# Last batch's tail in a gated cross-attention and mixture-of-experts kernel: the residual update moved from VectorE to ScalarE and GpSimd

## The chip, the cores and the metric

The kernel runs on one core of a Trainium2 chip, as one launch. The metric is the device time in microseconds (us), as the median of a few runs. TensorE is called PE below, VectorE DVE, ScalarE ACT, GpSimd POOL and SyncE SP, as the profile calls them.

## What is computed

Four batches of 512 tokens with 512 features go through a gated cross-attention to 64 context tokens, and then through a router and a mixture of 8 experts, of which each token takes 2. The part around the change is the end of the attention block and the start of the router:

```python
delta = ctx @ Wo.T + bo                      # [512 tokens, 512]
delta = rs * delta
delta = (delta - mean) / sqrt(var + EPS) * ln_gamma + ln_beta
x1 = x + tanh(g_xattn) * delta               # residual: stored, the output starts from it
h = (x1 - mean(x1)) / sqrt(var(x1) + EPS)    # second layer norm: stored, experts gather it
logits = h @ gate_weight.T                   # [2048, 8], top 2 of 8 follow
out = x1 + tanh(g_ffn) * experts(h)          # only after all 2048 tokens are routed
```

## The kernel before

The kernel is written engine by engine, with semaphores; each engine runs its list in the order written. Batches 0 to 3 go through attention in a software pipeline, in which the output of batch b-1 is finished while batch b's scores are computed. The last batch (`LAST`, 3) has nothing behind it: its four tiles of 128 tokens (t = 0 to 3) go through a **tail**, in which the engines hand each tile on to each other:

1. PE makes `delta` in a PSUM bank (`last_o_product`), then is done with it.
2. DVE, in `update_and_residual(n, u, r, last)`: for tile u, `bn_stats` and `bn_aggr` of `delta`, then `dh = (delta - mean) * gamma` (semaphore `dgam`; this is the line L459). For tile r, one `scalar_tensor_tensor` (L435) `xr = dh * rs + xs` (`x1_done`), then `bn_stats` (L439) and the variance of `xr` (`hvar`, L449). `xs` holds x + beta. One call does u = t and r = t - 1.
3. POOL: `inverse_delta(t)` is a power, `rs = (var + eps)^-1/2` (L812); `inverse_h(t)` is the same for the second norm (`rsh`, L816) and `nmh = -mean * rsh` (L819, semaphore `hbias`). `last_x_beta(t)` adds beta to x in `xs` (L891).
4. ACT, `normalise_h`: `dh = xr * rsh + nmh` (L1040, `h_done`).
5. PE, `h_transposes`: four 128x128 transposes of `dh` (L1409, `h_tr`).
6. ACT, `h_copy`: the transposed tile from PSUM to `ht` (L1047, `h_ev`).
7. PE, `router`: eight small matmuls `ht` by `gate_w` (L1415, `lg_mm`); a copy of the 8 logits follows (`keep_logits`, on DVE for the last batch, L464, on ACT for the others, L1052).

Between these steps PE runs `stay_busy(n)`: n transposes of the identity into a bank that nobody reads (L1303), 6 between a tile's transposes and its router, 12 behind each router but the last, 22 behind the last.

Behind the tail comes the routing. DVE picks the two best experts of each token in a chain of small instructions on 128x128 elements (from L643 on). ACT first splits three of expert 0's weight pieces (`first_gu`, L1216), whose weights were loaded meanwhile, and then computes the exponential that DVE's `wden` (L661) waits for. Slots are placed, the first rows are gathered by DMA, and then 37 slot tiles go through the experts' matmuls (L259) in a loop that takes the rest of the time.

SP stores x1 and h of each tile as they are done. Its `stores(n)` waits for `x1_done` and `h_done` in turn.

Of the kernel before, what the change touches and what calls it, by code (L numbers as in the profile page):

```python
# [4 lines left out]
ALU = mybir.AluOpType  # L5
ACT = mybir.ActivationFunctionType
# [9 lines left out]
NB = 4  # L16
# [27 lines left out]
def flamingo_gated_block(nc, x, ctx_t, mask, w_attn, b_cols, b_rows, gates, gate_t, w_exp, out):  # L44
    st = ExitStack()
    with st:
# [3 lines left out]
        def sem(name):  # L50
            return st.enter_context(nc.semaphore(name))
# [177 lines left out]
        o_l2, last_xb = sem("o_lo_second_half_done"), sem("last_x_with_beta")  # L229
        d_mm, dstats, dmean, dvar, drstd, dgam, xb_done, x1_done = (sem(n) for n in  # L230
# [54 lines left out]
        def _(sp):  # L285
# [13 lines left out]
            def stores(n):  # L299
                for t in range(TT):  # L300
                    sp.wait_ge(x1_done, n * TT + t + 1)
                    sp.dma_start(out_rows[n * TT + t], xr[:, t, :]).then_inc(x1_store[t], 16)
                    sp.wait_ge(h_done, n * TT + t + 1)
                    sp.dma_start(h_rows[n * TT + t], dh[:, t, :]).then_inc(h_store[t], 16)
# [24 lines left out]
            stores(LAST)  # L329
# [21 lines left out]
        def _(dve):  # L351
# [72 lines left out]
            def update_and_residual(n, u, r, last=False):  # L424
                delta = None if u is None else tail_bank[u] if last else bank[2 + u % 2]

                if r is not None:
                    dve.wait_ge(dgam, n * TT + r + 1)
                    dve.wait_ge(drstd, n * TT + r + 1)
                    if last:  # L430
                        dve.wait_ge(last_xb, r + 1)
                        dve.wait_ge(x1_store[r], 16 * NB)
                    else:
                        dve.wait_ge(xb_done, n * TT + r + 1)
                    dve.scalar_tensor_tensor(out=xr[:, r, :], in0=dh[:, r, :], scalar=rs[:, r:r + 1],  # L435
                                             in1=(xs if last else xr)[:, r, :],
                                             op0=ALU.mult, op1=ALU.add).then_inc(x1_done, 1)
                    dve.wait_ge(x1_done, n * TT + r + 1)
                    dve.bn_stats(st6h[:, r, :], xr[:, r, :]).then_inc(hstats, 1)  # L439
# [169 lines left out]
            for t in range(TT + 1):  # L609
                update_and_residual(LAST, t if t < TT else None, t - 1 if t > 0 else None, last=True)  # L610
# [155 lines left out]
        def _(pool):  # L766
# [43 lines left out]
            def inverse_delta(n, t):  # L810
                pool.wait_ge(dvar, n * TT + t + 1)
                pool.tensor_tensor(rs[:, t:t + 1], ve[:, t:t + 1], mhalf[:, 0:1], ALU.pow).then_inc(drstd, 1)  # L812
# [105 lines left out]
            for t in range(TT + 1):  # L918
                if t < TT:
                    inverse_delta(LAST, t)  # L920
                if t >= 1:
                    inverse_h(LAST, t - 1)
                if t < 2:
                    last_x_beta(t + 2)
# [62 lines left out]
        def _(act):  # L987
# [49 lines left out]
            def normalise_h(n, t):  # L1037
                act.wait_ge(x1_done, n * TT + t + 1)
                act.wait_ge(hbias, n * TT + t + 1)
                act.activation(dh[:, t, :], xr[:, t, :], ACT.Identity, scale=rsh[:, t:t + 1],  # L1040
                               bias=nmh[:, t:t + 1]).then_inc(h_done, 1)
# [169 lines left out]
            keep_logits(LAST - 1, 2)  # L1211
            h_copy(LAST - 1, 3)
# [9 lines left out]

            for t in range(TT):
                normalise_h(NB - 1, t)
                h_copy(NB - 1, t, tail=True)
# [70 lines left out]
        def _(pe):  # L1296
# [264 lines left out]
            for t in range(TT):  # L1561
                h_transposes(NB - 1, t, tail=True)
                stay_busy(6, tail_bank[0])
                router(NB - 1, t, tail=True)
                if t < TT - 1:
                    stay_busy(12, tail_bank[0])
# [120 lines left out]
```

## Time and profile before

| | us |
|---|---|
| median of 3 runs | 956.95 (953.62 to 959.67) |
| the profiled execution | 953.08 |
| its span, first to last instruction | 951.3 |
| PE busy | 904.9 (95%) |
| DVE busy | 432.6 (45%) |
| ACT busy | 383.4 (40%) |
| POOL busy | 267.8 (28%) |
| mean granted TensorE clock | 0.987 of full |

The page divides the span into 40 slices of 23.8 us. The tail, 219 to 240 us, lies in the tenth slice and the first part of the eleventh, and the routing in the rest of the eleventh and the twelfth. PE's busy digits are 7 to 9 in the first ten slices, 6 in the eleventh, and 9 from the twelfth on, but for the last. The granted clock, in tenths of full speed (9 is 90% or more), is 7 in the eleventh slice and in the last one, and 9 in all others. Busy time of PE contains the identity transposes, so it doesn't say how much of it is work.

### The profile page before, as it was taken

The page shows a single profiled execution, that of the slowest core. Times are in us where ns is not written, and L with a number is a line of the kernel's source. Part 1 is how long each engine was busy: PE and PEld are TensorE (multiplying, and loading weights), DVE is VectorE, ACT ScalarE, POOL GpSimd, SP SyncE. Part 2 cuts the span into 40 slices and gives each one's busy share as a digit, 9 for nine tenths or more (in the row PEclk, how much of TensorE's full clock was granted, in tenths as well). Part 3 has the DMA queues.
Part 4 walks back from the last instruction along what each step waited for, and adds up shares of the span by engine and source line. Part 5 has one row for each costly group of instructions (what it writes and reads, how often), then busy time and mean ns, then how long its engine had stood idle before and what let it go on. Part 6 is the DMA issues. An engine that isn't in the chain of part 4 may idle for free.

```text
span 951.3 us, 14769 instructions
## 1 busy us (share of the span) xinstructions
PE 904.9 (95%) x4369; PEld 726.9 (76%) x4370; DVE 432.6 (45%) x802; ACT 383.4 (40%) x740; POOL 267.8 (28%) x330
## 2 busy tenths in 40 slices
PE   7978999999699999999999999999999999999994
PEld 7746777778578888888888888888888888888883
DVE  5658868577871221721621635422532172136111
ACT  4485757543332222622622625322622262235221
POOL 6136555564412112212212212211311221212211
PEclk9999999999799999999999999999999999999997
DMA  8210222108272112631631543611551263121121
GB/s 315 90 45 1 78 100 77 56 34 314 99 288 44 23 22 37 208 109 33 203 117 33 189 131 110 221 22 22 170 161 22 37 213 103 33 33 22 33 33 22
DMA packets 27812, 92.90 MB, mean 98 GB/s; under 512 B 5457, under 2 KB 5457, under 8 KB 21137
## 3 DMA queue, kind: packets, MB, share of 16 engines
q1 hardware_dynamic: 18576, 72.03, 20.2%
q0 software_dynamic: 8640, 20.62, 11.8%
q8 instruction: 9, 0.15, 0.1%
q14 instruction: 11, 0.08, 0.0%
q10 hardware_dynamic: 576, 0.02, 0.0%
HBM read 73.98 MB, written 18.68 MB: 97 GB/s over the span
## 4 chain that ended last, share of the span: by engine, by line
PE 80%; issue 6%; POOL 5%; DVE 4%; ACT 3%; DMA 1%; DVEq 0%; SPq 0%; POOLq 0%; ACTq 0%
PE bank L259 71%; PE bank L1612 3%; PE bank L1598 2%; POOL ex_lo L824 2%; POOL o_lo L804 1%; DMA raw<-in_w_attn 1%; PE bank L1415 1%; PE bank L1303 1%; POOL xr L808 1%; ACT g_hi L1216 1%; PE bank L1409 1%; PE bank L1351 0%; DVE tok_tile L691 0%; DMA xg<-h_rows,slot_idx 0%; PE bank L1331 0%
## 5 line engine op out<-in xcount | busy, mean ns | idle before, releaser
L259 PE MATMUL bank<-g_hi,gt_hi 128*128 128x512 f32 x592 | 237.5, 401 | 0.9 <-DVE gt_lo L717 0.9
L259 PE MATMUL bank<-g_lo,gt_hi 128*128 128x512 f32 x592 | 234.1, 395 | 0.0
L259 PE MATMUL bank<-g_hi,gt_lo 128*128 128x512 f32 x592 | 234.1, 395 | 0.0
L747 DVE TENSOR_TENSOR hid<-silu,bank 128x256 f32<-128x256 f32 x148 | 61.4, 419 | 306.9 <-ACT silu L1268 306.9
L1268 ACT ACTIVATE silu<-bank 128x256 f32<-128x256 f32 x148 | 56.5, 382 | 253.0 <-PE bank L259 253.0
L966 POOL COPY g_idx<-slot_idx 128x1 int32 x37 | 6.9, 185 | 470.3 <-ACT w_nxt L1282 470.3
L259 PEld LDWEIGHTS bank<-g_hi,gt_lo 128*128 128x128 f32 x592 | 111.3, 188 | 27.0
L259 PEld LDWEIGHTS bank<-g_hi,gt_hi 128*128 128x128 f32 x592 | 111.3, 188 | 26.3 <-issue 1.1
L259 PEld LDWEIGHTS bank<-g_lo,gt_hi 128*128 128x128 f32 x592 | 111.4, 188 | 25.0
L259 PE MATMUL bank<-dn_hi,hd_hi 128*128 128x512 f32 x296 | 126.8, 428 | 0.0
L259 PE MATMUL bank<-dn_hi,hd_lo 128*128 128x512 f32 x296 | 116.9, 395 | 0.0
L259 PE MATMUL bank<-dn_lo,hd_hi 128*128 128x512 f32 x296 | 116.4, 393 | 0.0
L615 DVE TENSOR_TENSOR g_lo<-raw,g_hi 128x2048 fp32r<-128x2048 f32 x32 | 72.4, 2286 | 9.8 <-ACT g_hi L1216 9.7
L730 DVE TENSOR_TENSOR hd_lo<-bank,hd_hi 128x256 fp32r<-128x256 f32 x148 | 58.8, 418 | 36.2 <-ACT hd_hi L1251 36.2
L975 POOL DMA_INDIRECT out_rows<-y_sb,s_idx x37 | 59.1, 1597 | 41.7 <-ACT y_sb L1289 36.1
L1251 ACT ACTIVATE hd_hi<-bank 128x256 fp32r<-128x256 f32 x148 | 52.5, 384 | 42.1 <-PE bank L1612 42.1
L259 PEld LDWEIGHTS bank<-dn_hi,hd_lo 128*128 128x128 f32 x296 | 55.9, 189 | 13.8
L259 PEld LDWEIGHTS bank<-dn_lo,hd_hi 128*128 128x128 f32 x296 | 56.1, 189 | 8.1
L259 PEld LDWEIGHTS bank<-dn_hi,hd_hi 128*128 128x128 f32 x296 | 55.8, 189 | 8.0 <-issue 0.2
L824 POOL TENSOR_TENSOR ex_lo<-ex,ex_hi 128x512 fp32r<-128x512 f32 x32 | 43.8, 1387 | 63.9 <-ACT ex_hi L1064 30.3
L1216 ACT ACTIVATE g_hi<-raw 128x2048 fp32r<-128x2048 f32 x32 | 61.0, 1912 | 0.0
L946 POOL DMA_INDIRECT xg<-h_rows,g_idx x38 | 50.8, 1337 | 30.7 <-POOL g_idx L966 30.1
(236 smaller groups left out, 1284.8 us busy)
## 6 DMA issues: line engine op xcount, KB each, us to landing
raw<-in_w_exp SPq DMA_DIRECT2D x48, 1024.0 KB, 5.3
xs<-in_x SPq DMA_DIRECT2D x4, 1024.0 KB, 6.3
out_rows<-xr SPq DMA_DIRECT2D x16, 256.0 KB, 2.1
h_rows<-dh SPq DMA_DIRECT2D x16, 256.0 KB, 2.1
raw<-in_w_attn SPq DMA_DIRECT2D x3, 1024.0 KB, 14.0
xr<-in_x SPq DMA_DIRECT2D x3, 1024.0 KB, 5.8
raw<-in_w_attn SPq DMA_DIRECT2D x4, 256.0 KB, 7.2
rows<-in_b_rows SPq DMA_DIRECT2D x1, 1024.0 KB, 17.6
```

The source lines that it names most:

```text
L259: mm = eng.matmul(psum, a(k), b(k), start=(first and k == 0 and j == 0), stop=(last and k == n - 1 and j == 2))
L615: dve.tensor_tensor(dst.rearrange("p k n -> p (k n)"), raw[:, p, :], f32(hi.rearrange("p k n -> p (k n)")), ALU.subtract).then_inc(done, 1)
L730: dve.tensor_tensor(hd_lo[:, 2 * p:2 * p + 2, :].rearrange("p k n -> p (k n)"), bank[4 + p % 2][:, 0:256], f32(hd_hi[:, 2 * p:2 * p + 2, : ...
L747: dve.tensor_tensor(hid[:, p, :], silu[:, p, :], bank[p][:, 256:512], ALU.mult).then_inc(hid_done, 1)
L824: pool.tensor_tensor(ex_lo[:, s % RING, :], ex[:, s % 2, :], f32(ex_hi[:, s % RING, :]), ALU.subtract).then_inc(e_l, 1)
L946: pool.indirect_dma_start(out=xg[:, 0:HW], out_offset=None, in_=h_dram[:, :], in_offset=bass.IndirectOffsetOnAxis(ap=rows, axis=0)).then_i ...
L975: pool.indirect_dma_start(out=out[:, :], out_offset=bass.IndirectOffsetOnAxis(ap=s_idx[:, 0:1], axis=0), in_=y_sb[:, :], in_offset=None, c ...
L1216: act.activation(dst.rearrange("p k n -> p (k n)"), raw[:, p, :], ACT.Copy).then_inc(done, 1)
L1251: act.activation(hd_hi[:, 2 * p:2 * p + 2, :].rearrange("p k n -> p (k n)"), bank[4 + p % 2][:, 0:256], ACT.Copy).then_inc(hd_h, 1)
L1268: act.activation(silu[:, p, :], bank[p][:, 0:256], ACT.Silu).then_inc(silu_done, 1)
L1598: tr = pe.transpose(bank[6][:, k * P:(k + 1) * P], xg[:, k * P:(k + 1) * P], ident[:, :])
L1612: tr = pe.transpose(bank[4 + p % 2][:, c * P:(c + 1) * P], hid[:, p, c * P:(c + 1) * P], ident[:, :])
```

## The change

- The last batch's `xr = dh * rs + xs` is no longer one DVE instruction. ACT does `dh = dh * rs` in place (`scale_update(t)`, semaphore `last_scaled`), then POOL does `xr = dh + xs` (`last_add(t)`, semaphore `last_x1`). DVE's statistics of `xr` wait for `last_x1`, and so do ACT's `normalise_h` and SP's store.
- On DVE one call now does u = t and r = t - 2, instead of t - 1, in six calls instead of five.
- On ACT `scale_update(0)` and `scale_update(1)` stand among the last steps of the batch before, and `scale_update(t + 2)` between `h_copy(t)` and `normalise_h(t + 1)`.
- On POOL the four `last_add` are put between the powers, and `last_x_beta(2)` and `(3)` move.
- PE no longer runs the 12 identity transposes behind each of the first three routers (36 in all). The 6 ahead of each router and the 22 behind the last stay.
- The first three batches compute as before.

```diff
@@ vector: update_and_residual @@
-                if r is not None:
+                if r is not None and last:
+                    dve.wait_ge(last_x1, r + 1)
+                if r is not None and not last:
                     dve.wait_ge(dgam, n * TT + r + 1)
                     dve.wait_ge(drstd, n * TT + r + 1)
-                    if last:
-                        dve.wait_ge(last_xb, r + 1)
-                        dve.wait_ge(x1_store[r], 16 * NB)
-                    else:
-                        dve.wait_ge(xb_done, n * TT + r + 1)
+                    dve.wait_ge(xb_done, n * TT + r + 1)
                     dve.scalar_tensor_tensor(out=xr[:, r, :], in0=dh[:, r, :], scalar=rs[:, r:r + 1],
-                                             in1=(xs if last else xr)[:, r, :],
-                                             op0=ALU.mult, op1=ALU.add).then_inc(x1_done, 1)
+                                             in1=xr[:, r, :], op0=ALU.mult, op1=ALU.add).then_inc(x1_done, 1)
                     dve.wait_ge(x1_done, n * TT + r + 1)
+                if r is not None:
                     dve.bn_stats(st6h[:, r, :], xr[:, r, :]).then_inc(hstats, 1)
...
-            for t in range(TT + 1):
-                update_and_residual(LAST, t if t < TT else None, t - 1 if t > 0 else None, last=True)
+            for t in range(TT + 2):
+                update_and_residual(LAST, t if t < TT else None, t - 2 if t > 1 else None, last=True)
@@ gpsimd @@
-            for t in range(TT + 1):
-                if t < TT:
-                    inverse_delta(LAST, t)
-                if t >= 1:
-                    inverse_h(LAST, t - 1)
-                if t < 2:
-                    last_x_beta(t + 2)
+            def last_add(t):
+                pool.wait_ge(last_scaled, t + 1)
+                pool.wait_ge(x1_store[t], 16 * NB)
+                pool.wait_ge(last_xb, t + 1)
+                pool.tensor_tensor(xr[:, t, :], dh[:, t, :], xs[:, t, :], ALU.add).then_inc(last_x1, 1)
...
@@ scalar @@
+            def scale_update(t):
+                act.wait_ge(dgam, LAST * TT + t + 1)
+                act.wait_ge(drstd, LAST * TT + t + 1)
+                act.activation(dh[:, t, :], dh[:, t, :], ACT.Copy, scale=rs[:, t:t + 1]).then_inc(last_scaled, 1)
...
             keep_logits(LAST - 1, 2)
+            scale_update(0)
             h_copy(LAST - 1, 3)
             keep_logits(LAST - 1, 3)
...
+            scale_update(1)
+            normalise_h(LAST, 0, True)
             for t in range(TT):
-                normalise_h(NB - 1, t)
-                h_copy(NB - 1, t, tail=True)
+                h_copy(LAST, t, tail=True)
+                if t + 2 < TT:
+                    scale_update(t + 2)
+                if t < TT - 1:
+                    normalise_h(LAST, t + 1, True)
@@ tensor @@
                 stay_busy(6, tail_bank[0])
                 router(NB - 1, t, tail=True)
-                if t < TT - 1:
-                    stay_busy(12, tail_bank[0])
             stay_busy(22, bank[7])
```

Two pieces of the order in which instructions stand on their engines follow, each before and after. Line numbers of the changed kernel are higher by 14 to 27. A row has the line, the operation, what is written from what, the size, and the semaphores waited for.

ACT before, from the logits of the batch before's tile 2 (`logits` is `keep_logits`, `ht` is `h_copy`, `dh<-xr,nmh,rsh` is `normalise_h`) to the first weight split:

```order
L1052 ACTIVATE logits<-bank0 128x8 [waits logits_product]
L1047 ACTIVATE ht<-bank1 128x512 [waits h_transposed]
L1052 ACTIVATE logits<-bank1 128x8 [waits logits_product]
L1040 ACTIVATE dh<-xr,nmh,rsh 128x512 [waits h_bias,x1_done]
L1047 ACTIVATE ht<-bank0 128x512 [waits h_transposed]
L1040 ACTIVATE dh<-xr,nmh,rsh 128x512 [waits h_bias,x1_done]
L1047 ACTIVATE ht<-bank1 128x512 [waits h_transposed]
L1040 ACTIVATE dh<-xr,nmh,rsh 128x512 [waits h_bias,x1_done]
L1047 ACTIVATE ht<-bank2 128x512 [waits logits_product,h_transposed]
L1040 ACTIVATE dh<-xr,nmh,rsh 128x512 [waits h_bias,x1_done]
L1047 ACTIVATE ht<-bank3 128x512 [waits logits_product,h_transposed]
L1216 ACTIVATE g_hi<-raw 128x2048 [waits raw_piece0_loaded,delta_product]
```

ACT now, from the same place to the last batch's `normalise_h` of tile 2 (`dh<-dh,rs` is `scale_update`):

```order
L1073 ACTIVATE logits<-bank0 128x8 [waits logits_product]
L1056 ACTIVATE dh<-dh,rs 128x512 [waits delta_rstd,delta_gamma]
L1068 ACTIVATE ht<-bank1 128x512 [waits h_transposed]
L1073 ACTIVATE logits<-bank1 128x8 [waits logits_product]
L1056 ACTIVATE dh<-dh,rs 128x512 [waits delta_rstd,delta_gamma]
L1061 ACTIVATE dh<-xr,nmh,rsh 128x512 [waits h_bias,last_x1_done]
L1068 ACTIVATE ht<-bank0 128x512 [waits h_transposed]
L1056 ACTIVATE dh<-dh,rs 128x512 [waits delta_rstd,delta_gamma]
L1061 ACTIVATE dh<-xr,nmh,rsh 128x512 [waits h_bias,last_x1_done]
L1068 ACTIVATE ht<-bank1 128x512 [waits h_transposed]
L1056 ACTIVATE dh<-dh,rs 128x512 [waits delta_rstd,delta_gamma]
L1061 ACTIVATE dh<-xr,nmh,rsh 128x512 [waits h_bias,last_x1_done]
```

The scaling of tile 0 stands behind the logits of the batch before's tile 2. The scalings of tiles 2 and 3 stand behind the copies of tiles 0 and 1, each ahead of the next tile's `normalise_h`.

POOL before, from `inverse_delta` of the last batch's tile 0 on (`rs` is `inverse_delta`, `rsh` and `nmh` are `inverse_h`, `xs` is `last_x_beta`):

```order
L812 TENSOR_TENSOR rs<-ve,mhalf 128x1 [waits delta_var]
L891 TENSOR_TENSOR xs<-xs,rows 128x512 [waits hs_done]
L812 TENSOR_TENSOR rs<-ve,mhalf 128x1 [waits delta_var]
L816 TENSOR_TENSOR rsh<-veh,mhalf 128x1 [waits h_var]
L819 TENSOR_SCALAR nmh<-mvh,rsh 128x1 [waits h_rstd,attn_weights0_loaded]
L891 TENSOR_TENSOR xs<-xs,rows 128x512 [waits hs_done]
L812 TENSOR_TENSOR rs<-ve,mhalf 128x1 [waits delta_var]
L816 TENSOR_TENSOR rsh<-veh,mhalf 128x1 [waits h_var]
L819 TENSOR_SCALAR nmh<-mvh,rsh 128x1 [waits h_rstd,attn_weights0_loaded]
L812 TENSOR_TENSOR rs<-ve,mhalf 128x1 [waits delta_var]
L816 TENSOR_TENSOR rsh<-veh,mhalf 128x1 [waits h_var]
L819 TENSOR_SCALAR nmh<-mvh,rsh 128x1 [waits h_rstd,attn_weights0_loaded]
```

POOL now, from `inverse_delta` of tile 1 on (`xr<-dh,xs` is `last_add`; the `inverse_h` of tiles 2 and 3 follow):

```order
L814 TENSOR_TENSOR rs<-ve,mhalf 128x1 [waits delta_var]
L925 TENSOR_TENSOR xr<-dh,xs 128x512 [waits last_x_with_beta,x1_tile0_stored,last_update_scaled]
L893 TENSOR_TENSOR xs<-xs,rows 128x512 [waits hs_done]
L925 TENSOR_TENSOR xr<-dh,xs 128x512 [waits last_x_with_beta,x1_tile1_stored,last_update_scaled]
L818 TENSOR_TENSOR rsh<-veh,mhalf 128x1 [waits h_var]
L821 TENSOR_SCALAR nmh<-mvh,rsh 128x1 [waits h_rstd,attn_weights0_loaded]
L814 TENSOR_TENSOR rs<-ve,mhalf 128x1 [waits delta_var]
L925 TENSOR_TENSOR xr<-dh,xs 128x512 [waits last_x_with_beta,x1_tile2_stored,last_update_scaled]
L818 TENSOR_TENSOR rsh<-veh,mhalf 128x1 [waits h_var]
L821 TENSOR_SCALAR nmh<-mvh,rsh 128x1 [waits h_rstd,attn_weights0_loaded]
L814 TENSOR_TENSOR rs<-ve,mhalf 128x1 [waits delta_var]
L925 TENSOR_TENSOR xr<-dh,xs 128x512 [waits last_x_with_beta,x1_tile3_stored,last_update_scaled]
```

The `inverse_h` of tile 0 now stands behind the adds of tiles 0 and 1, that of tile 1 behind the add of tile 2, and that of tile 2 behind the add of tile 3.

## Rows read from the trace of the kernel before

**Rows 1.** Chain that ended last, 222 to 247 us: start, us, engine, tile and line.
```profile
228.25 2.65 PE bank L1303 x12
...
236.71 1.36 PE bank L1303 x12
...
239.04 5.50 ACT g_hi L1216 x3
...
244.75 0.18 DVE wden L661
```

**Rows 2.** Timeline of PE in the tail: start, us, instruction, count, [idle before it].
```profile
225.56 0.66 PE L1409 MATMUL bank<-ident,dh 128*128 128x128 f32 x4 [0.97 <-ACT dh L1040]
...
235.65 1.06 PE L1415 MATMUL bank<-gate_w,ht 128*128 128x8 f32 x8
...
237.91 0.60 PE L1409 MATMUL bank<-ident,dh 128*128 128x128 f32 x4
...
239.20 1.06 PE L1415 MATMUL bank<-gate_w,ht 128*128 128x8 f32 x8
```

**Rows 3.** Timeline of ACT in the tail, with the batch before's last steps.
```profile
219.12 0.81 ACT L1040 ACTIVATE dh<-xr,nmh,rsh 128x512 f32<-128x512 f32 x1
222.39 0.18 ACT L1052 ACTIVATE logits<-bank 128x8 f32<-128x8 f32 x1 [2.46 <-PE bank L1415]
222.88 0.60 ACT L1047 ACTIVATE ht<-bank 128x512 f32<-128x512 f32 x1 [0.31 <-PE bank L1409]
...
224.70 0.81 ACT L1040 ACTIVATE dh<-xr,nmh,rsh 128x512 f32<-128x512 f32 x1
226.26 0.60 ACT L1047 ACTIVATE ht<-bank 128x512 f32<-128x512 f32 x1 [0.75 <-PE bank L1409]
227.65 0.81 ACT L1040 ACTIVATE dh<-xr,nmh,rsh 128x512 f32<-128x512 f32 x1 [0.80 <-POOL nmh L819]
...
238.55 0.60 ACT L1047 ACTIVATE ht<-bank 128x512 f32<-128x512 f32 x1 [2.25 <-PE bank L1409]
```

**Rows 4.** Timeline of DVE from the last batch's tile 0 on.
```profile
218.99 1.72 DVE L435 SCALAR_TENSOR_TENSOR xr<-dh,rs,xs 128x512 f32<-128x512 f32 x1
220.74 0.70 DVE L439 BATCH_NORM_STATS2 st6h<-xr 128x6 f32<-128x512 f32 x1
...
222.14 0.15 DVE L449 TENSOR_SCALAR veh<-mvh 128x1 f32<-128x1 f32 x1
...
223.31 0.75 DVE L435 SCALAR_TENSOR_TENSOR xr<-dh,rs,xs 128x512 f32<-128x512 f32 x1
...
240.29 0.17 DVE L464 COPY logits<-bank 128x8 f32<-128x8 f32 x1 [3.38 <-PE bank L1415]
```

**Rows 5.** Timeline of POOL in the tail.
```profile
218.86 1.29 POOL L891 TENSOR_TENSOR xs<-xs,rows 128x512 f32<-128x512 f32 x1
...
223.19 0.55 POOL L816 TENSOR_TENSOR rsh<-veh,mhalf 128x1 f32<-128x1 f32 x1
223.91 0.29 POOL L819 TENSOR_SCALAR nmh<-mvh,rsh 128x1 f32<-128x1 f32 x1 [0.17 <-POOL rsh L816]
```

**Rows 6.** Groups of ACT instructions by shape: count, busy us and mean ns.
```profile
L1088 ACT ACTIVATE ex_hi<-ex 128x512 fp32r<-128x512 f32 x18 | 11.4, 632 | 0.7
```

**Rows 7.** Stretches: length, busy us (count) of PE, PEld, DVE, ACT, POOL, then granted clock, DMA.
```profile
224.10:227.52 3.42, 2.42 (x21) 2.09 (x20) 3.27 (x9) 1.48 (x3) 2.63 (x5) 1.00 1.02 424
227.52:230.94 3.42, 3.42 (x18) 3.42 (x19) 3.27 (x9) 0.81 (x1) 1.38 (x4) 0.50 1.04 402
...
254.85:258.30 3.45, 2.74 (x16) 1.53 (x16) 3.45 (x21) 0.00 (x0) 2.96 (x6) 0.50 0.00 0
258.30:261.70 3.40, 3.40 (x19) 3.11 (x20) 2.74 (x11) 0.00 (x0) 1.31 (x1) 0.51 0.00 0
261.70:265.10 3.40, 2.35 (x21) 2.07 (x20) 2.96 (x5) 0.39 (x1) 0.00 (x0) 1.00 0.28 78
```

**Rows 8.** Chain at the start of the experts' loop: 12 matmuls in a row.
```profile
275.66 2.81 PE bank L259 x12
```

More of the change, by code:

```diff
@@ L229, in flamingo_gated_block @@
         o_l2, last_xb = sem("o_lo_second_half_done"), sem("last_x_with_beta")
+        last_scaled, last_x1 = sem("last_update_scaled"), sem("last_x1_done")
         d_mm, dstats, dmean, dvar, drstd, dgam, xb_done, x1_done = (sem(n) for n in
@@ L297, in _, with stores @@
             sp.dma_start(raw[:, 3, :], w_attn[3]).then_inc(wload[3], 16)
-            def stores(n):
+            def stores(n, last=False):
                 for t in range(TT):
-                    sp.wait_ge(x1_done, n * TT + t + 1)
+                    if last:
+                        sp.wait_ge(last_x1, t + 1)
+                    else:
+                        sp.wait_ge(x1_done, n * TT + t + 1)
                     sp.dma_start(out_rows[n * TT + t], xr[:, t, :]).then_inc(x1_store[t], 16)
@@ L328, in _ @@
                 sp.dma_start(raw[:, p, :], w_exp[0, p]).then_inc(raw_in[p], 16)
-            stores(LAST)
+            stores(LAST, True)
             for t in range(TT):
@@ L917, in _ @@
             inverse_h(LAST - 1, 3)
-            for t in range(TT + 1):
-                if t < TT:
-                    inverse_delta(LAST, t)
-                if t >= 1:
-                    inverse_h(LAST, t - 1)
-                if t < 2:
-                    last_x_beta(t + 2)
+            def last_add(t):
[3 more added lines that the diff above has]
+                pool.tensor_tensor(xr[:, t, :], dh[:, t, :], xs[:, t, :], ALU.add).then_inc(last_x1, 1)
+            inverse_delta(LAST, 0)
+            last_x_beta(2)
+            inverse_delta(LAST, 1)
+            last_add(0)
+            last_x_beta(3)
+            last_add(1)
+            inverse_h(LAST, 0)
+            inverse_delta(LAST, 2)
+            last_add(2)
+            inverse_h(LAST, 1)
+            inverse_delta(LAST, 3)
+            last_add(3)
+            inverse_h(LAST, 2)
+            inverse_h(LAST, 3)
             pool.wait_ge(rt, weight_step[0])
@@ L1035, in o_high, with normalise_h @@
                 act.activation(o_hi[:, m, :], o_un[:, m, :], ACT.Copy).then_inc(o_h, 1)
-            def normalise_h(n, t):
-                act.wait_ge(x1_done, n * TT + t + 1)
+            def scale_update(t):
+                act.wait_ge(dgam, LAST * TT + t + 1)
+                act.wait_ge(drstd, LAST * TT + t + 1)
+                act.activation(dh[:, t, :], dh[:, t, :], ACT.Copy, scale=rs[:, t:t + 1]).then_inc(last_scaled, 1)
+            def normalise_h(n, t, last=False):
+                act.wait_ge(*((last_x1, t + 1) if last else (x1_done, n * TT + t + 1)))
                 act.wait_ge(hbias, n * TT + t + 1)
```

## The prediction

> **What bounds the kernel now.** I read the chain of waits first, around the tail. From 222 to 240 us it runs nearly all on PE, and much of it is not work: behind the router of tile 0 it holds 12 identity transposes of 2.65 us, behind each of the next two 12 of 1.36 us (the last of them stands) [rows 1]. Then it goes to ACT, whose three weight splits take 5.50 us from 239.04 on, and to DVE's `wden` at 244.75. Everything up to the experts' loop follows from there in one string.
>
> In PE's timeline [rows 2] one tile is transposes (237.91), 6 fillers and the wait for ACT's copy to 239.20, then the router. PE was idle 0.97 us before tile 0's transposes (225.56), as `normalise_h` came late; from then on it never waited for ACT's normalisation.
>
> ACT [rows 3] copies tile 3 at 238.55 and begins its splits 0.49 later. DVE [rows 4] gets tile 3's logits at 240.29; `wden` is 4.46 behind that and 6.20 behind ACT's copy, and both roads arrive at almost the same time (the exponential needs both). So what counts is how far the last `h_copy` and the last router move; the later road decides.
>
> **What the change removes.** 36 fillers, 2.65 + 1.36 + 1.36 = 5.4 us of the chain. If everything else had kept its pace, the last `normalise_h` would have come by DVE's and POOL's old pace: DVE's L435 stands at 218.99 and 223.31 for tiles 0 and 1, the second 0.75 long and the first, which met POOL's add of 218.86, 1.72 [rows 4, 5]. The distance of 4.32 less that stall of 0.97 is 3.35 a tile, so tile 3's would start at 230.0. From L435 to `veh`'s end it is 3.3 less the same stall, 2.3; `inverse_h` (1.1, below) brings tile 3's `normalise_h` to 233.5, and 1.56 more its copy to 235.1. That is 3.5 us earlier than 238.55: the most that the fillers' removal can bring.
>
> **What it adds, and where.** The update takes a way over two more engines. I work through the tail with these pieces:
> - `scale_update`, 128x512 SBUF to SBUF on ACT, isn't in the trace. The nearest are the plain copy `ex_hi`, 632 ns [rows 6], below, and `dh<-xr,nmh,rsh` with two column operands, 0.81 [rows 3], above. It has one such operand: 0.75.
> - `last_add` is the same shape and operation as `last_x_beta`, 1.29 [rows 5].
> - `inverse_h`, from its start at 223.19, ends at 223.91 + 0.29 = 224.20; with the hop to ACT of about 0.1 it costs 1.10 [rows 5].
> - `normalise_h` to the start of `h_copy`: 224.70 to 226.26, 1.56 [rows 3]. `h_copy` holds ACT for 0.49.
> - A hop between engines: the rows show 0.03 (router's end 240.26 to the logits' copy at 240.29) and 0.05 (`normalise_h`'s end 225.51 to PE's 225.56) [rows 2 to 4]; over POOL and DVE I take 0.08.
>
> *Tile 0.* Before, DVE began L435 at 218.99. Now ACT must scale it first, and `scale_update(0)` stands behind the logits copy that waits for PE until 222.39 [rows 3]. It runs from 222.5 to 223.25. `last_add(0)` is 223.3 to 224.6, then `last_x_beta(3)` to 225.9. `scale_update(0)` also delays the other batch's `h_copy` from 222.88 to 223.2, and thus its router and the logits copy, behind which `normalise_h(0)` began at 224.70 before, to about 225.0; `scale_update(1)` ends at 225.8. `last_add(1)` is 225.9 to 227.2. Only now comes `inverse_h(0)` in POOL's queue (DVE was ready at 226.3: 1.55 from `bn_stats` to `veh` [rows 4]). `normalise_h(0)` starts at 228.3, where it was 224.70: 3.6 later.
>
> *The ring.* From here the orders of ACT and POOL close a ring. `normalise_h(0)`, `h_copy(0)`, then `scale_update(2)`, `last_add(2)`, and only behind it `inverse_h(1)`, for which `normalise_h(1)` waits; and so again for tile 3. One round: 1.56 + 0.49 + 0.75 + 0.08 + 1.29 + 1.10 = 5.3 us. A tile before cost PE 3.55 (router 235.65 to router 239.20) [rows 2]. Statistics two tiles ahead don't help, since `inverse_h` doesn't wait for DVE but for its place in POOL's queue. So `normalise_h(1)` is at 233.6 and `normalise_h(2)` at 238.8, `h_copy(2)` at 240.4, `normalise_h(3)` (its `nmh` is ready by 239.9) at 240.9, and `h_copy(3)` at 242.5. Against 238.55 that is **3.9 us later**, at full clock.
>
> *The clock.* The granted clock was 1.00, 2.4 GHz, in the stretch from 224.10 to 227.52, in which PE stood idle for 0.97 us, and 0.50, 1.2 GHz, in the next, in which it never stopped; behind that one 12 fillers take 1.36 again [rows 1, 7]. Ahead of the loop it was at 0.50 twice, first with PE stopping between small matmuls, then without a stop, and at 1.00 behind that. So in these rows it came back only behind work without a gap. Now PE is idle from about 224.9 to 229.1 and again between tiles, with nothing to fill it, and I take it to be at 1.2 GHz for most of the tail. The price is in the fillers: 12 took 2.65 instead of 1.36, 0.22 each instead of 0.11. A tile's four transposes cost 0.4 more and are on the path each time; the router's eight cost 0.9 and the six fillers 0.7 more. With that `transposes(2)` start at 240.3, and PE's own work of tile 2 (0.9, 1.3 and 1.8) holds `transposes(3)` until 244.3. They end at 245.1, the six fillers at 246.4, the router (1.8, and 0.2 to its last end) at 248.4. Logits at 248.4 against 240.29 are **8.2 later**; ACT's road is 6.7 later.
>
> **The sum.** 3.9 if the clock stays full, 8.2 if it is low all along. I take 7.0, nearer the second, since all of PE's stops speak for it, with a round or so at full clock. By a scale of 0.63 or 0.81 each the sum is 0.4 less or 0.3 more. DVE's stall by POOL and its four L435 (1.72 + 3 x 0.75 = 4.0 us) go, but DVE isn't on the path any more, so that counts nothing. SP's stores come later with the tiles; only the gather, well behind `wden`, waits for them. The weights that ACT splits at 239.04 were not waited for, and are needed later now. What is behind `wden` moves as it is.
>
> The profiled execution took 953.08, 1.8 around its span of 951.3; so it would be 960.1. The median of the three runs is 3.9 above the profiled one, 956.95, and I predict in its terms: **964.0 us**.
>
> **Rivals.**
>
> *Full clock.* The ring is right, but PE's clock doesn't fall or is back soon: +3.9, 960.9. For it: the clock came back ahead of tile 1 before [rows 7]. Against it: PE had fillers then that are now gone. The Trainium skill, "TensorE: Matmul & The Clock Gate", Part 4, says that transposes don't count as PE-busy in the same way. By that rule the 36 fillers held no clock, and taking them away costs none: this rival's 960.9. The trace goes against it: the clock came back at about 230.9, after a stretch whose 2.65 us of fillers are transposes [rows 1, 7]. The same page, "What's actually happening", has the clock gated to 1.2 GHz when PE is idle; by that it would be 965.2, my sum at low clock. 15%.
>
> *The fillers were the bound, and the new way is hidden.* The copy of tile 3 comes at 235.1, -3.5, 953.5. It would need `normalise_h(1)` before 230 us, that is ACT and POOL giving tile 0 back in under 2 us after 228.3, against 5.3 by rows; or `scale_update(0)` starting near 219 instead of 222.5. For it is only that the chain now is on PE [rows 1]. It decides if PE still never waits for `normalise_h`. 8%.
>
> *The low clock reaches beyond the tail.* The last 22 fillers at 0.22 are 4.9 us, 0.4 more than the 4.46 from the logits to `wden`, and DVE waits for counting matmuls behind them: 0.5. If PE is still low when the loop starts, its first group of 12 matmuls, 2.81 [rows 8], takes twice that; half may be hidden by DVE's splits, which the group also waits for: 1.4. With 8.2 that gives +10.1, 967.1. Before, the clock was also low ahead of the loop and back for it, 0.51 until 261.70 and 1.00 behind [rows 7], so most likely it is so again. 15%.
>
> **Chances and range.** The forecast has 62%. Its own range, from the clock returning in one round to none, is 961 to 966.5. Runs of one kernel here differ by 3 us to either side, and 1% (9.6 us) is about what can be told from no change. Slower by over 1% is the last rival and the upper edge of the forecast, 0.20; faster by over 1% needs more than the second rival has, 0.02; within 1% 0.78. The range leaves out that second rival and little else, with 3 us for the runs: 958 to 970.
>
> **What would show it.** On ACT: `scale_update(0)` at about 222.5, `normalise_h(LAST, 0)` near 228.3, then distances of 5.3 to 5.8 between the next two, each waiting for POOL. On POOL: `last_add(2)` waiting for ACT, with `inverse_h(1)` right behind. On PE: idle some 4 us before tile 0's transposes, and again before tiles 1 and 2; granted clock 0.5 in most of 228 to 248 us. `wden` at about 252. I am wrong if PE has no gaps there, if `normalise_h(0)` comes before 226, or if `wden` is before 245.

## The result, and the profile after

Over 18 runs of each kernel the changed one took 960.29 us in the median (959.48 to 965.28) and the one before 957.34 (952.41 to 960.33). The ratio is 1.0049, with a 95% interval of 1.0034 to 1.0064: slower by 0.5%, 4.7 us. It is not the quotient of the two medians, which are 2.95 us or 0.3% apart. The profiled execution took 960.12 with a span of 958.3, against 953.08 and 951.3 before: 7.0 us.

The part of the chain that answers to [rows 1], from the page's chain view of the changed kernel (start, us, engine, tile, line):

```profile
223.38 1.26 POOL xr L925
...
225.87 1.22 POOL xr L925
227.09 0.52 POOL rsh L818
...
228.13 0.82 ACT dh L1061
228.99 1.13 PE bank L1436 x4
...
230.64 0.72 ACT dh L1056
231.43 1.26 POOL xr L925
232.69 0.52 POOL rsh L818
...
233.73 0.82 ACT dh L1061
...
246.33 1.52 PE bank L1442 x8
...
252.24 0.19 DVE wden L663
```

The chain no longer stays on PE with its fillers. It goes POOL, ACT, PE, ACT, POOL and round again: normalise (L1061), transposes (L1436), the tile's copy and the next scaling (L1068, L1056), add (L925), power (L818). That is the ring.

ACT's timeline of the changed kernel, beside [rows 3] (start, us, line, instruction, what ended the wait before it):

```profile
219.23 0.81 ACT L1061 ACTIVATE dh<-xr,nmh,rsh 128x512 f32<-128x512 f32 x1
222.50 0.18 ACT L1073 ACTIVATE logits<-bank 128x8 f32<-128x8 f32 x1 [2.46 <-PE bank L1442]
222.57 0.72 ACT L1056 ACTIVATE dh<-dh,rs 128x512 f32<-128x512 f32 x1
...
228.13 0.81 ACT L1061 ACTIVATE dh<-xr,nmh,rsh 128x512 f32<-128x512 f32 x1 [2.41 <-POOL nmh L821]
...
230.64 0.71 ACT L1056 ACTIVATE dh<-dh,rs 128x512 f32<-128x512 f32 x1
233.73 0.81 ACT L1061 ACTIVATE dh<-xr,nmh,rsh 128x512 f32<-128x512 f32 x1 [2.38 <-POOL nmh L821]
...
239.34 0.81 ACT L1061 ACTIVATE dh<-xr,nmh,rsh 128x512 f32<-128x512 f32 x1 [2.38 <-POOL nmh L821]
241.35 0.60 ACT L1068 ACTIVATE ht<-bank 128x512 f32<-128x512 f32 x1 [1.21 <-PE bank L1436]
...
245.09 0.60 ACT L1068 ACTIVATE ht<-bank 128x512 f32<-128x512 f32 x1 [2.44 <-PE bank L1436]
```

The scaling of tile 0 begins behind the logits copy, at 222.57, though its input was ready near 219. The normalisation of tile 0 starts at 228.13, where it was 224.70, and the next ones follow at 5.60 and 5.61, each after a wait of 2.4 us for POOL's `nmh`. POOL in turn waits for ACT (beside [rows 5]):

```profile
227.04 0.55 POOL L818 TENSOR_TENSOR rsh<-veh,mhalf 128x1 f32<-128x1 f32 x1
...
231.43 1.26 POOL L925 TENSOR_TENSOR xr<-dh,xs 128x512 f32<-128x512 f32 x1 [2.89 <-ACT dh L1056]
232.65 0.55 POOL L818 TENSOR_TENSOR rsh<-veh,mhalf 128x1 f32<-128x1 f32 x1
```

The add of tile 2 waits 2.89 us for its scaling, and tile 1's `rsh` runs behind it, at 232.65, though DVE had its variance at 228.68. PE's waits and the granted clock of the same stretches, beside [rows 2] and [rows 7] (the stretches' columns are busy us of PE, PEld, DVE, ACT, POOL, then the clock and DMA):

```profile
228.99 1.11 PE L1436 MATMUL bank<-ident,dh 128*128 128x128 f32 x4 [4.11 <-ACT dh L1061]
...
234.60 1.11 PE L1436 MATMUL bank<-ident,dh 128*128 128x128 f32 x4 [1.71 <-ACT dh L1061]
```

```profile
227.52:230.94 3.42, 1.95 (x9) 1.95 (x10) 2.06 (x7) 1.61 (x3) 0.85 (x3) 0.50 1.06 426
...
244.60:248.00 3.40, 3.40 (x19) 3.40 (x18) 0.12 (x1) 2.91 (x3) 0.00 (x0) 0.50 0.00 0
...
251.40:254.85 3.45, 3.07 (x39) 2.69 (x37) 3.03 (x14) 2.02 (x2) 1.09 (x2) 1.00 0.95 401
```

PE is idle 4.11 and 1.71 us ahead of tiles 0 and 1, and 1.70 ahead of tile 2, and at 1.2 GHz (0.50) from about 227 until 251, when the last 22 fillers are nearly through.

### The profile page after: what moved, and what is told of

Same layout as the page of the kernel before. It is cut to its first block, busy times and chain, and to the rows that moved or that the text cites. A ratio compares the mean times of both kernels' runs of the same rounds, so it can differ in the third digit from the quotient of the medians.

```text
span 958.3 us, 14701 instructions
## 1 busy us (share of the span) xinstructions
PE 908.6 (95%) x4333; PEld 731.3 (76%) x4334; DVE 427.9 (45%) x798; ACT 386.4 (40%) x744; POOL 273.0 (28%) x334
## 4 chain that ended last, share of the span: by engine, by line
PE 78%; POOL 6%; issue 6%; DVE 5%; ACT 2%; DMA 1%; DVEq 0%; SPq 0%; POOLq 0%; ACTq 0%
PE bank L260 69%; PE bank L1637 3%; PE bank L1623 2%; POOL ex_lo L826 2%; POOL o_lo L806 1%; DMA raw<-in_w_attn 1%; POOL xr L810 1%; PE bank L1330 1%; PE bank L1436 1%; PE bank L1442 1%; POOL xr L925 1%; PE bank L1378 0%; POOL rs L814 0%; DVE xr L437 0%; PE bank L1358 0%
```

## Experiments

The kernels start the tail a little earlier or later from run to run, by up to 3.6 us in these traces. So I measure it by a distance: from the batch before's last `normalise_h` (219.12 in the trace before) to `wden`. All times in us, ratios against the runs of the kernel before that were made beside each:

| kernel | last `normalise_h` to `wden` | median | ratio (95%) |
|---|---|---|---|
| before | 25.6 | 957.34 | |
| before, second trace | 29.6 | one run, 958.18 | |
| changed | 33.0 | 960.29 | 1.0049 (1.0034 to 1.0064) |
| only_update | 32.1 | 959.11 | 1.0063 (1.0045 to 1.0081) |
| only_fillers | 25.95 | 953.72 | 0.9996 (0.9977 to 1.0015) |
| ring_open | 29.8 | 957.48 | 1.0044 (1.0023 to 1.0065) |
| scale_early | 30.0 | 957.47 | 1.0020 (0.9996 to 1.0045) |
| ring_warm | 29.2 | 956.40 | 1.0011 (0.9993 to 1.0029) |
| open_warm | 23.9 | 952.06 | 0.9966 (0.9947 to 0.9986) |
| gap_filled | 24.0 | 951.38 | 0.9960 (0.9944 to 0.9976) |
| beta_early_filled | 20.9 | 950.23 | 0.9942 (0.9922 to 0.9963) |
| beta_late_filled | 21.0 | 948.97 | 0.9928 (0.9901 to 0.9955) |

The runs of the kernel before had a median of 957.34 beside the changed kernel, 954.04 beside `only_update`, `only_fillers` and `ring_open`, 956.66 beside `scale_early`, `ring_warm`, `gap_filled` and `beta_early_filled`, and 954.37 beside the other two. So ratios of different groups can be set against each other only to about 0.002: `ring_open` and `scale_early` have the same median and ratios of 1.0044 and 1.0020.

The theory is the prediction's: the update's move delays tile 0 and closes a ring (3.9 us), and PE's idle time lowers its clock (up to 4.3 more). The main rival was that the loss is the clock that the removed fillers had held, and nothing else.

**The kernel before once more.** No edit.

> The kernel before once more, for a second trace of it: its runs spread from 952.4 to 960.3 us where those of the changed kernel lie closely around 960. The ring says nothing on that. If the spread comes from TensorE's clock, this trace, when it is slower than 951.3 us of span, has 1.2 GHz in stretches of the tail or the routing where the first trace had 2.4, and differs there by as much; tiles' normalisations stay where they were (224.7 us for tile 0).

Its stretches (start:end, length, busy us, clock):

```profile
227.52:230.94 3.42, 3.42 (x19) 3.42 (x18) 3.28 (x9) 1.41 (x2) 1.40 (x4) 0.50 1.00 424
230.94:234.35 3.41, 3.41 (x18) 3.41 (x17) 2.25 (x6) 0.02 (x1) 1.92 (x5) 0.50 1.01 306
...
237.77:241.20 3.43, 3.40 (x22) 3.16 (x21) 0.00 (x0) 0.87 (x2) 0.00 (x0) 0.70 0.39 148
```

The fillers behind the routers of tiles 1 and 2, from its chain:

```profile
237.09 2.65 PE bank L1303 x12
...
242.03 1.36 PE bank L1303 x12
```

PE never stops behind 227.5, as in [rows 7], but it stays at 1.2 GHz until about 240, where the first trace had 2.4 from 231 on. So the fillers, which never stop, can themselves run at half speed, and here they do so behind the routers of tiles 0 and 1, where the first trace had it behind the first alone. Tile 0 is normalised at 5.58 behind the batch before's last, as in the first trace (224.70 less 219.12); `wden` is 4.0 later by distance. The stop of 0.97 us ahead of tile 0 is the same in both, but the clock fell 1.9 us behind it in the first trace and within it in this one (at about 226.2, the stop being 225.9 to 226.9). The runs of the kernel before bear this out. Of 19 on one chip the fastest took 952.0 at a mean granted clock of 0.988, the slowest 959.7 at 0.973, and those between lie nearly in that order (954.0 at 0.983, 957.6 at 0.977). The kernel before has a time that goes with how long the clock is low; that it is the tail's clock which differs, this one trace shows, and `gap_filled` below bears it out. The changed one's 18 runs had 0.966 to 0.977, all at the low end.

**Each half of the change alone.** `only_update` puts the fillers back:

```diff
                 router(NB - 1, t, tail=True)
+                if t < TT - 1:
+                    stay_busy(12, tail_bank[0])
             stay_busy(22, bank[7])
```

> The changed kernel with the 36 identity transposes behind the routers put back, so only the update's move is left. Ring: a round takes 5.3 to 5.6 us as in the changed kernel, the first normalisation starts at 228.1; the last copy of a tile is 4 us (full clock) to 8.5 us (low clock, the 12 fillers of 0.22 us being then in the way of the next transposes) behind that of the kernel before, so the kernel is as slow as the changed one or slower, 1.004 to 1.009 of before. Rival (the loss is the clock that the fillers held): with them back it is at the time before, ratio 1.000, within 0.2%.

ACT's `dh<-xr,nmh,rsh` of the last batch's tiles 1 and 2 (tile 0's is at 227.80):

```profile
233.41 0.81 ACT L1061 ACTIVATE dh<-xr,nmh,rsh 128x512 f32<-128x512 f32 x1 [2.38 <-POOL nmh L821]
...
239.71 0.81 ACT L1061 ACTIVATE dh<-xr,nmh,rsh 128x512 f32<-128x512 f32 x1 [2.39 <-POOL nmh L821]
```

The ratio is 1.0063, and the intervals of this and the changed kernel overlap. The rounds are 5.61 and 6.30, the second longer because the fillers at half speed held the transposes. By distance 6.5 of the changed kernel's 7.4 us come with the update's move alone; the rival falls. Taking the fillers out as well adds 0.9 us between two single traces, and nothing that the ratios can tell.

`only_fillers` is the kernel before without its 36 fillers:

```diff
                 router(NB - 1, t, tail=True)
-                if t < TT - 1:
-                    stay_busy(12, tail_bank[0])
```

> The kernel before without the 36 identity transposes, the update left on VectorE. Ring: there is none here, tiles follow at VectorE's pace of 3.35 us; the last copy is at about 235.1 us (before 238.55), and wden 1.5 (low clock: transposes, 6 fillers and the last router cost 2.0 more) to 3.5 us earlier than in the trace of before, ratio 0.996 to 0.999. Rival (the loss is the clock that the fillers held): wden 4 us or more later, ratio 1.004 or more, as in the changed kernel.

The ratio, 0.9996, shows no change, and `wden` came 0.3 later by distance where I had expected it 1.5 to 3.5 earlier. ACT's copies of the four tiles, at 227.28, 231.02, 234.75 and 238.48, show why; two of them:

```profile
231.02 0.60 ACT L1047 ACTIVATE ht<-bank 128x512 f32<-128x512 f32 x1 [2.00 <-PE bank L1409]
...
234.75 0.60 ACT L1047 ACTIVATE ht<-bank 128x512 f32<-128x512 f32 x1 [2.37 <-PE bank L1409]
```

They stand 3.73 apart. I had priced the low clock for the last tile only. But at 1.2 GHz four transposes, six fillers and a router are 3.73 of PE's own work, more than DVE's 3.35, and PE sets the pace for every tile. The clock was at 0.50 from about 226 to 246. The rival had wanted `wden` 4 us later, and that didn't come either.

**Opening the ring.** `ring_open` has the instructions of the changed kernel in another order:

```diff
@@ vector @@
-            for t in range(TT + 2):
-                update_and_residual(LAST, t if t < TT else None, t - 2 if t > 1 else None, last=True)
+            for t in range(TT):
+                update_and_residual(LAST, t, None, last=True)
+            for t in range(TT):
+                update_and_residual(LAST, None, t, last=True)
@@ gpsimd @@
             inverse_delta(LAST, 1)
+            inverse_delta(LAST, 2)
             last_add(0)
+            inverse_delta(LAST, 3)
             last_x_beta(3)
             last_add(1)
             inverse_h(LAST, 0)
-            inverse_delta(LAST, 2)
             last_add(2)
             inverse_h(LAST, 1)
-            inverse_delta(LAST, 3)
             last_add(3)
@@ scalar @@
-            scale_update(1)
+            for t in range(1, TT):
+                scale_update(t)
             normalise_h(LAST, 0, True)
             for t in range(TT):
                 h_copy(LAST, t, tail=True)
-                if t + 2 < TT:
-                    scale_update(t + 2)
```

> The changed kernel with the same instructions in another order: VectorE does all four updates before the first statistics of x1, ScalarE scales tiles 1 to 3 before the first normalisation, GpSimd does its four powers for them early, so that no scaling waits for an earlier tile's copy; the fillers stay out. Ring: normalisations follow at GpSimd's pace of 2.2 us (one add and one inverse_h), at about 228.7, 231.0, 233.2 and 234.8; the last copy at 236.8 instead of 245.1, wden 7 to 8 us earlier than in the changed kernel, ratio to before 0.997 to 1.000. Rivals (the low clock, or the adds being on GpSimd at all, is what costs): it stays within 2 us of the changed kernel, ratio 1.003 to 1.005.

By distance it gained 3.2 us on the changed kernel, less than half of what I expected, and its ratio of 1.0044 is the rivals'. POOL's adds and powers went as expected, but PE did not keep up (the add of tile 2, then the transposes of tiles 1 and 2):

```profile
229.07 1.26 POOL L927 TENSOR_TENSOR xr<-dh,xs 128x512 f32<-128x512 f32 x1
```

```profile
233.83 1.09 PE L1437 MATMUL bank<-ident,dh 128*128 128x128 f32 x4
...
237.56 1.10 PE L1437 MATMUL bank<-ident,dh 128*128 128x128 f32 x4
```

```profile
234.35:237.77 3.42, 3.42 (x18) 3.42 (x17) 0.02 (x1) 1.29 (x2) 0.26 (x1) 0.50 0.98 368
```

The add of tile 2 is at 229.07 and that of tile 3 2.17 behind it; the transposes are 3.73 apart, with PE never waiting, at half speed. I had left out the price of the low clock for every tile, as in `only_fillers`. With the ring open PE at 1.2 GHz is the next bound, so this run couldn't tell the ring from the clock. The next two kernels do, by holding the clock.

**Holding the clock, the ring left closed.** `ring_warm` fills PE's waits in the changed kernel:

```diff
             router(LAST - 1, 3)
+            stay_busy(34, tail_bank[0])
             for t in range(TT):
                 h_transposes(NB - 1, t, tail=True)
                 stay_busy(6, tail_bank[0])
                 router(NB - 1, t, tail=True)
+                if t < 2:
+                    stay_busy(25, tail_bank[0])
```

> The changed kernel with identity transposes put where TensorE was idle: 34 ahead of tile 0, 25 behind the routers of tiles 0 and 1, sized to end as the next transposes can start; none of them is in the way. Ring with the clock as its second term: granted clock 2.4 GHz through the tail, rounds of 5.2 to 5.3 instead of 5.6, the last copy 2.6 us and wden 3.6 us earlier than in the changed kernel's trace (3.9 us behind the trace of before); ratio to before 1.000 to 1.004. Rival (all of the loss is the clock): rounds of 3.5 us and a ratio of 1.000 or less. If the clock falls all the same, the fillers are twice as long and in the way, and it is slower than the changed kernel by 3 us or more.

```profile
233.11 0.81 ACT L1061 ACTIVATE dh<-xr,nmh,rsh 128x512 f32<-128x512 f32 x1 [2.39 <-POOL nmh L821]
...
238.26 0.81 ACT L1061 ACTIVATE dh<-xr,nmh,rsh 128x512 f32<-128x512 f32 x1 [2.38 <-POOL nmh L821]
```

```profile
234.35:237.77 3.42, 3.39 (x31) 3.15 (x30) 0.51 (x1) 1.21 (x2) 1.78 (x2) 1.00 0.61 234
```

The clock was 2.4 GHz throughout the tail, to 251 us, and the rounds are 5.15: the ring without the clock. `wden` lies 3.6 behind the first trace of before by distance (29.2 less 25.6), where 3.9 was worked out, and 3.8 ahead of the changed kernel. So against that trace the two terms are about equal, 3.6 of tile 0's wait and the ring, and 3.8 of clock. With the ratio of 1.0011 the kernel can't be told from the one before, whose runs have their own low clock in them.

**Holding the clock, the ring open.** `open_warm` is `ring_open` with one line more:

```diff
             router(LAST - 1, 3)
+            stay_busy(38, tail_bank[0])
```

> ring_open with 38 identity transposes ahead of tile 0, where TensorE was idle for 4.6 us; so the update is on ScalarE and GpSimd, the ring is open and the clock is held. Expected: 2.4 GHz through the tail, normalisations 2.2 us apart (one add and one inverse_h on GpSimd), from the batch before's last normalisation to wden 23.5 us, where ring_open had 29.8, the changed kernel 33.0 and the kernel before 25.6; ratio to before 0.995 to 0.998. Rival (the adds on GpSimd cost more than these two causes): 26 us or more, ratio 1.000 or above.

The distance is 23.9, 5.9 less than `ring_open` with the same instructions and order on the other engines, and 5.3 less than `ring_warm`, where the ring is closed at the same clock. ACT's normalisations are 2.16 and 2.17 apart:

```profile
233.97 0.81 ACT L1063 ACTIVATE dh<-xr,nmh,rsh 128x512 f32<-128x512 f32 x1
...
236.14 0.81 ACT L1063 ACTIVATE dh<-xr,nmh,rsh 128x512 f32<-128x512 f32 x1
```

```profile
234.35:237.77 3.42, 3.39 (x31) 3.15 (x31) 1.27 (x5) 1.79 (x3) 2.33 (x5) 1.00 0.98 335
```

Ring and clock together are the change's loss. With the ring open and the clock held the way is 9.1 shorter than the changed kernel's. Scaling on ACT and adding on POOL cost nothing then, and gain nothing: `gap_filled` below, which leaves the update on DVE, has 24.0.

**Tile 0's late start.** `scale_early` moves two scalings of the changed kernel:

```diff
+            scale_update(0)
+            scale_update(1)
             keep_logits(LAST - 1, 2)
-            scale_update(0)
             h_copy(LAST - 1, 3)
             keep_logits(LAST - 1, 3)
...
-            scale_update(1)
             normalise_h(LAST, 0, True)
```

> The changed kernel with scale_update of tiles 0 and 1 both ahead of the logits copy that waits for TensorE until 222.4 us; all else as changed. Ring: the two scalings start at about 220.0 and 220.9, the adds of tiles 0 and 1 end by 224.6, the first normalisation starts at 225.6 instead of 228.1, the rounds behind it stay at 5.6, and wden comes 2.5 us earlier than in the changed kernel; ratio to before between 0.0025 and 0.003 lower than the changed one's. Rival (tile 0's late start is hidden by TensorE or the low clock): wden within 0.5 us of the changed kernel's distance from the batch before.

```profile
219.72 0.71 ACT L1056 ACTIVATE dh<-dh,rs 128x512 f32<-128x512 f32 x1
...
225.33 0.81 ACT L1061 ACTIVATE dh<-xr,nmh,rsh 128x512 f32<-128x512 f32 x1 [0.64 <-POOL nmh L821]
...
230.47 0.81 ACT L1061 ACTIVATE dh<-xr,nmh,rsh 128x512 f32<-128x512 f32 x1 [2.37 <-POOL nmh L821]
```

Tile 0 is normalised 6.3 behind the batch before's last, where the changed kernel took 8.9: the 2.6 us that `scale_update(0)` and `(1)` had waited behind the logits copies. The distance fell by 3.0, the rest because tile 0's transposes were still at full clock. The median is 2.8 lower than the changed kernel's, with that of the kernel before 0.7 lower beside it. The ratio is 0.0029 lower, which the intervals alone would not carry. The rounds are 5.1 and 5.6, as a closed ring has them.

**The kernel before, its own gap filled.**

```diff
             router(LAST - 1, 3)
+            stay_busy(8, tail_bank[0])
```

> The kernel before with 8 identity transposes more, in the 0.97 us in which TensorE waited for tile 0's normalisation; nothing else. If the low clock in the tail of the kernel before comes from that gap: granted clock 2.4 GHz through the tail, the 12 fillers behind tile 0 take 1.36 instead of 2.65, wden 1.3 us earlier than in the first trace of before and 4 to 5 us earlier than in the second; runs no longer spread up to 960, median 951 to 952.5 us, ratio 0.997 or less. Rival (the clock falls for another reason, such as the work of all that stretch being small matmuls): spread and median as before, ratio 1.000, the 8 fillers then costing up to 0.9.

```profile
227.52:230.94 3.42, 3.39 (x31) 3.15 (x30) 3.27 (x9) 1.41 (x2) 1.35 (x3) 1.00 1.02 419
230.94:234.35 3.41, 3.38 (x31) 3.14 (x30) 1.38 (x6) 1.52 (x3) 1.10 (x3) 1.00 0.96 300
```

```profile
228.12 1.51 PE L1303 MATMUL bank<-ident 128*128 128x128 f32 x12
```

Eight transposes of nothing, in 0.97 us of waiting, gave 0.4%: 951.38, and a spread of 950.45 to 952.22 over 12 runs where the kernel before had 952.02 to 960.70 beside it. The 12 fillers behind tile 0 take 1.51 in the timeline, at full speed. So the low clock in the tail of the kernel before came from that gap. The kernel before at full clock is then 24.0 by distance, and against it the changed kernel loses 9.0: 5.2 by tile 0's wait and the ring (`ring_warm`, 29.2) and 3.8 by the clock. The 3.6 found above was smaller because the first trace of before had some low clock of its own.

**Versions meant to beat both.** `beta_early_filled` leaves the update on DVE, takes the 36 fillers out, and puts 8 ahead of tile 0 and 6 behind tile 1's router. It moves POOL's adds of beta, so that none meets DVE's first update, which [rows 4, 5] show at 1.72 beside POOL's add:

```diff
@@ gpsimd @@
+            last_x_beta(0)
+            last_x_beta(1)
             for m in range(KC):
                 pool.wait_ge(o_h, NT + m + 1)
...
             inverse_h(LAST - 1, 1)
-            last_x_beta(0)
+            last_x_beta(2)
             inverse_delta(LAST - 1, 3)
             inverse_h(LAST - 1, 2)
-            last_x_beta(1)
+            last_x_beta(3)
...
-                if t < 2:
-                    last_x_beta(t + 2)
@@ tensor @@
             router(LAST - 1, 3)
+            stay_busy(8, tail_bank[0])
...
                 router(NB - 1, t, tail=True)
-                if t < TT - 1:
-                    stay_busy(12, tail_bank[0])
+                if t == 1:
+                    stay_busy(6, tail_bank[0])
```

> A version meant to beat both: the update left on VectorE as before, the 36 fillers out, 8 fillers ahead of tile 0 and 6 behind the router of tile 1 in TensorE's waits, and GpSimd's four adds of beta moved one place earlier each pair, the first two into its idle time at 201 us, so that none meets VectorE's first update (1.72 us becomes 0.75). If the clock stays at 2.4 GHz: copies of the tiles at about 226.3, 228.3, 231.4 and 233.7, wden 4.9 us earlier than in the first trace of before, ratio 0.993 to 0.996. If the clock is low all the same: wden 1.5 to 2.5 us earlier, ratio 0.997 to 0.999.

```profile
203.14 0.76 DVE L414 TENSOR_SCALAR r_two<-rden 48x256 fp32r<-48x256 f32 x1
203.93 1.37 DVE L416 TENSOR_TENSOR r_two<-rden,r_two 48x256 fp32r<-48x256 f32 x1
...
221.50 0.75 DVE L435 SCALAR_TENSOR_TENSOR xr<-dh,rs,xs 128x512 f32<-128x512 f32 x1
```

The distance is 20.9, 4.7 less than in the first trace of before and 3.0 less than `gap_filled`, and DVE's update takes 0.75. Of the 3.0 about 1.0 is the shorter update, by DVE's rows (1.72 less 0.75); the other 2, by subtraction, is my estimate of what the 36 fillers cost at full clock. But two of the moved adds, at 202.5, met two other DVE instructions. The first, which took 0.28 before, took 0.76, and the second 1.37 instead of 0.42; both are on the path. `beta_late_filled` therefore leaves the adds where the kernel before had them and lets the third wait until the update has passed:

```diff
@@ gpsimd @@
                 if t < 2:
+                    if t == 0:
+                        pool.wait_ge(x1_done, LAST * TT + 1)
                     last_x_beta(t + 2)
```

> Like beta_early_filled, but GpSimd's four adds of beta stay where the kernel before had them, and the third alone waits until VectorE has made tile 0's x1. In beta_early_filled the two adds moved to 202.5 us met two VectorE instructions on 48x256 elements, which took 0.76 and 1.37 us instead of 0.28 and 0.42, 1.4 us on the path. Ring and the port: those take 0.28 and 0.42 again, tile 0's update still takes 0.75, the distance from the batch before's last normalisation to wden stays 20.9 us, and the time is 1.4 us under beta_early_filled's, ratio 0.9925 to 0.9935. Rival (the update's 1.72 us had another cause than GpSimd's add): it takes 1.7 again and the kernel is 1 us slower than that.

```profile
205.46 0.29 DVE L414 TENSOR_SCALAR r_two<-rden 48x256 fp32r<-48x256 f32 x1
205.78 0.42 DVE L416 TENSOR_TENSOR r_two<-rden,r_two 48x256 fp32r<-48x256 f32 x1
...
222.40 0.75 DVE L435 SCALAR_TENSOR_TENSOR xr<-dh,rs,xs 128x512 f32<-128x512 f32 x1
```

All three are short. It is the fastest of all, 948.97 us, 0.9928 of before, over 6 runs from 948.28 to 951.28. Its interval overlaps that of `beta_early_filled`, so that the last 1.3 us rest on the trace: from the first of the three instructions to the third it is 16.9 us, where `beta_early_filled` has 18.4. The Trainium skill, "SBUF — State Buffer", section "SBUF: two separate sides", has a port pair that VectorE and GpSimd share, locked for a whole instruction against VectorE instructions with two SBUF inputs or in a 2-port mode. The rows agree for the two with two inputs (1.72, 1.37); which mode the 0.76 one was in no run shows.

## Why the prediction was right, and by how much not

I predicted 964.0 us, slower but within 1%. It is 960.3, slower by 0.49% (0.3% by the medians), inside the range but 3.7 us under the forecast.

| step | worked out | changed kernel's trace |
|---|---|---|
| `scale_update(0)` starts, takes | 222.5, 0.75 | 222.57, 0.72 |
| `last_add(0)` starts, takes | 223.3, 1.29 | 223.37, 1.27 |
| `normalise_h(0)` | 228.3 | 228.13 |
| a round | 5.3, up to 0.4 more at low clock | 5.60 |
| `h_copy(3)` | 242.5 to 245.3 | 245.09 |
| last logits | 244.2 to 248.4 | 247.88 |
| `wden` | about 252 | 252.24 |

- **The ring**: right. `open_warm` against `ring_warm` opens it at full clock and gains 5.3 us, though tile 0 is normalised 0.5 later there (9.5 against 8.9 behind the batch before's last): from there to the last copy it is 8.3 instead of 14.1.
- **Tile 0's wait behind the logits copy**: right, 2.6 us (`scale_early`).
- **The clock**: right in kind. I took it to be low in most rounds with one at full; it was low in all of them, the upper bound of the sum. By distance the loss is 7.4 us, 8.2 worked out for that bound: I had priced PE's own work at 1.2 GHz at 4.0 a tile, and it is 3.73. That the sum of 7.0 meets the 7.0 of the two profiled executions so closely is luck, as it took a round at full clock that didn't come.
- **What counts at nothing**: from `wden` to the experts' first matmul it is 21.3 us in the changed kernel and 21.4 before, so nothing came behind the tail and the third rival didn't occur. DVE's freed 4 us brought nothing.
- **The step that failed** is the last: "The median of the three runs is 3.9 above the profiled one, 956.95, and I predict in its terms". In the profiled executions the difference was 7.0, as summed, and 960.1 was worked out for the profiled one, which took 960.12. But the 3.9 is not noise around both. It is the same low clock in the tail, which the kernel before had for only 3.4 us in its trace and for 13.6 in `before_again` (+4.0 by distance). Of its 18 runs beside the changed kernel 14 lie above 955.8; their clocks are not on record, so that this was the clock in them too is argued from the other runs. Adding the full price of the clock to a median that already held part of it counted that part twice: the changed kernel's median is 960.29, where its profiled run took 960.12, so nearly nothing was to be added. The difference came out as 4.7 by the ratio and not 7.0.
- **The second rival** fell. Its 3.5 us hold only at full clock: without fillers alone the kernel before gains nothing (`only_fillers`), since PE at 1.2 GHz has 3.73 us of own work a tile; with the clock held and the update's stall gone as well it gains 4.7 by distance (`beta_early_filled`).

What stays open is why the clock falls and comes back at different times in different runs of the kernel before; no run here tells that. And the early scaling was only tried with the ring closed and at low clock.

## What to carry to other kernels

When a step is spread over more engines, write down for each engine what stands ahead of it in its queue, and look for a path from a tile's step back to the next tile's: if ACT scales tile t + 2 only behind tile t's copy, and POOL's power for tile t + 1 only behind tile t + 2's add, running ahead on a third engine helps nothing. Before a term is added to a median, ask what makes the runs of the kernel spread; here the mean granted clock of each run said it. And a filler is worth its place only where the engine waits: eight in a wait of 0.97 us gave 0.4%. Thirty-six where it did not wait brought nothing at low clock, and cost about 2 us, by my estimate, once the clock was held.

## What the hardware showed

- With a stop of 0.97 us in a stretch of transposes and 8-column matmuls PE was at 1.2 GHz in the tail of the kernel before; with the stop filled by identity transposes all stretches of the tail were at 2.4 GHz (`gap_filled`). Behind it PE never stopped, and the clock was back by 231 us in one trace of that kernel and by 240 in the other. The length of a stop alone doesn't tell it: in the first trace PE then stood idle for 2.07 us ahead of 244.78, and the clock was at 1.00 until about 251.
- Identity transposes hold the clock: in `ring_warm` PE ran nothing else in the waits of the tail, 34 in a row from 224.56 on, and the clock stayed at 1.00 from 224 to 251 us. The rule on transposes that the prediction names from the Trainium skill ("TensorE: Matmul & The Clock Gate", Part 4) doesn't hold for these.
- ACT's scaling of 128x512 from SBUF to SBUF takes 0.72 us, between the plain copy's 0.63 [rows 6] and the 0.81 with scale and bias; POOL's add of two such tiles 1.27.
